# A selective scan in units: one ring of three PSUM tiles for units and side jobs, and stores begun by ScalarE

## What is computed

```
dA = exp(dl[..., None] * A)
h  = dA * h + (dl * ul)[..., None] * Bl[:, :, None, :]
y  = einsum('bkdn,bkn->bkd', h, Cl)      # over 4096 positions in order
```

## Time and profile before

| | |
|---|---|
| median of 3 runs | 11577.95 us (11575.34 to 11589.02) |
| profiled execution | 11574.58 us, its span 11572.8 us |
| first scan, end of last scan | 655.3 us, 9681.1 us |
| busy | VectorE 10116.4, TensorE 9678.0, GpSimd 9157.8, ScalarE 8511.6 us |
| mean granted TensorE clock | 0.957 of 2.4 GHz |

### The profile page before, as it was taken

The page is one execution under the profiler, slowest core; times in us unless marked ns, Lnnn a source line. Parts: engine busy times, 40 slices in busy tenths (PEclk is TensorE's granted clock), DMA queues, the critical chain, the costliest instruction groups (busy, mean ns, idle before and its releaser), DMA issues. The chain is left out here.

```text
span 11572.8 us, 332532 instructions
## 1 busy us (share of the span) xinstructions
PE 9678.0 (84%) x136268; PEld 6104.2 (53%) x136268; DVE 10116.4 (87%) x6303; ACT 8511.6 (74%) x15618; POOL 9157.8 (79%) x3978
## 2 busy tenths in 40 slices
PE   8967888788888788888787778888888887999999
PEld 5644444444444444444444444444444444788778
DVE  7879999999999999999999999999999996555554
ACT  3468888887888788878888888788888884444443
POOL 1169999998999899989999999899999996433330
PEclk9989999999999999999999999999999998999999
DMA  3366676676667766776677666666766674212210
GB/s 103 106 164 169 171 175 171 167 178 168 172 166 174 177 167 164 173 174 168 171 175 178 172 167 171 175 168 171 178 174 166 171 175 111 65 48 67 61 50 12
DMA packets 561649, 1716.32 MB, mean 148 GB/s; under 512 B 147138, under 2 KB 147938, under 8 KB 558344
## 3 DMA queue, kind: packets, MB, share of 16 engines
q1 hardware_dynamic: 560136, 1695.05, 58.4%
HBM read 1319.08 MB, written 375.39 MB: 146 GB/s over the span
## 5 line engine op out<-in xcount | busy, mean ns | idle before, releaser
L975 POOL TENSOR_TENSOR HC<-H,crep 128x1024 f32<-128x1024 f32 x3072 | 7201.2, 2376 | 583.8 <-PE psum L723 416.0
L797 DVE TENSOR_TENSOR_SCAN H<-E,car,psum 128x1024 f32<-128x1024 f32 x2112 | 4868.7, 2336 | 237.4 <-PE psum L701 113.3
L701 PE MATMUL psum<-diag,dluT 128*32 128x128 f32 x98304 | 3350.7, 288 | 1083.0 <-DVE H L797 1049.2
L701 PEld LDWEIGHTS psum<-diag,dluT 128*32 128x32 f32 x98304 | 2852.9, 116 | 2080.8 <-DVE H L797 1887.9
L882 ACT ACTIVATE E<-dlr,am 128x1024 f32<-128x1024 f32 x2816 | 3194.4, 1143 | 1001.7 <-DMA dlr<-scr_dl 519.4
L866 ACT ACTIVATE diag<-idn,blt 128x128 f32<-128x128 f32 x8192 | 2521.6, 389 | 119.8 <-PE psum L701 119.8
L723 PE MATMUL psum<-HC,sely 128*32 128x512 f32 x12288 | 2232.0, 620 | 32.6 <-POOL HC L975 30.9
L775 DVE TENSOR_TENSOR psum<-dur,psum 128x1024 f32<-128x1024 f32 x1280 | 1548.7, 1210 | 114.6 <-PE psum L664 90.4
L797 DVE TENSOR_TENSOR_SCAN H<-E,psum 128x1024 f32<-128x1024 f32 x704 | 1582.1, 2276 | 75.6 <-PE psum L701 45.9
L664 PE MATMUL psum<-sx,selb 96*128 96x512 f32 x2560 | 981.4, 465 | 532.4 <-DVE H L797 522.3
L664 PEld LDWEIGHTS psum<-sx,selb 96*128 96x128 f32 x2560 | 395.4, 190 | 1423.5 <-DVE H L797 1139.3
(11 more groups left out here) (143 smaller groups left out, 9796.9 us busy)
## 6 DMA issues: line engine op xcount, KB each, us to landing
dur<-scr_dlu SPq DMA_DIRECT2D x3072, 128.0 KB, 4.0
dlr<-scr_dl SPq DMA_DIRECT2D x3072, 128.0 KB, 3.8
crep<-scr_bc SPq DMA_DIRECT2D x1024, 256.0 KB, 5.2
scr_dlu<-dlu SPq DMA_DIRECT2D x256, 384.0 KB, 4.6
scr_yk<-yt SPq DMA_DIRECT2D x256, 384.0 KB, 3.0
brep<-scr_bc SPq DMA_DIRECT2D x512, 128.0 KB, 3.5
scr_dl<-dlt SPq DMA_DIRECT2D x128, 384.0 KB, 5.6
scr_dl<-yt SPq DMA_DIRECT2D x128, 384.0 KB, 3.3
```

The source lines that it names most:

```text
L701: r = e.matmul(P[un % 2][32 * q:32 * q + 32, i * 128:(i + 1) * 128], dluT[:, m % 2, i, 32 * j:32 * j + 32], diag[:, i, at + q, :], start=T ...
L797: e.tensor_tensor_scan(H[:, un % NH, ::step], decay[:, ::step], drive[:, ::step], init, ALU.mult, ALU.add).then_inc(scan_done)
L975: e.tensor_tensor(HC[:, un % NHC, :], H[:, un % NH, :], crep[:, GREP.index(g), :], ALU.mult).then_inc(hc_done)
```

## The change

Numbers are per step: x is the unit's place in it, n the step, c the next chunk.

- `yps` moves to the last two banks; the other six make three tiles P[0..2]. A list `ring` writes down the order in which TensorE takes tiles, for units and side jobs alike; a job takes tile (place % 3) and waits until the job three places earlier has released it (a unit by its scan, project by `split`, delta by dl, turn by its copy).
- TensorE fills unit un+2 in iteration un. Side jobs: project at x=4, deltas at 6 and 8 (before 7 and 10), turn at 1 in both steps (odd step before: 0). `turn_b` joins the turn of the even step, its output at column `BLT_AT`.
- ScalarE starts the DMAs of bc (x=6), dl (x=9 and 11 of the even step) and y (x=6) itself; `copy_y` moves from x=4 to 5, the first delta from 7 to 8, the copies of turn from 3 to 2 (even) and 1 to 4 (odd). `DIAGS` is dealt out anew; at the start 32 diags come ahead of exp 0.
- GpSimd's pooled multiply moves from x=11 to 9 (even) and 10 to 11 (odd), its delta of the odd step from 0 to 2.
- u is loaded in two halves of 384 KB, in the odd step after the one whose y is copied.
- SyncE's order is new.

```diff
-    DIAGS = (0, 0, 15, 3, 0, 8, 7, 0, 8, 3, 10, 0, 7, 3, 0, 0, 0, 0, 0, 0, 0, 0, 0, 0)
+    DIAGS = (0, 3, 8, 4, 3, 7, 17, 0, 0, 0, 11, 0, 9, 2, 0, 0, 0, 0, 0, 0, 0, 0, 0, 0)
+    NP = 3
+    BLT_AT = 448
+    FILL_AHEAD = 2
-    P = [psum[:, 0:1024], psum[:, 1024:2048]]
-    yps = psum[:, 2048:3072]
-    stage = psum[:, 3072:4096]
+    P = [psum[:, i * 1024:(i + 1) * 1024] for i in range(NP)]
+    yps = psum[:, 3072:4096]
...
+    def side_jobs(n, x):
         c = n // 2 + 1
+        jobs = []
         if n % 2 == 0:
+            if x == 1:
+                jobs += [("lt", n + 1)]
+            if x == 4 and c < NCHUNK:
+                jobs += [("x", c)]
+            if x == 6 and c < NCHUNK:
+                jobs += [("dt", 2 * c)]
+            if x == 8 and c < NCHUNK:
+                jobs += [("dt", 2 * c + 1)]
+        elif x == 1 and c < NCHUNK:
+            jobs += [("lt", 2 * c)]
+        return jobs
+
+    ring = [("x", 0), ("dt", 0), ("lt", 0), ("dt", 1)] + [("unit", un) for un in range(FILL_AHEAD)]
+    for un in range(NUNIT):
+        if un + FILL_AHEAD < NUNIT:
+            ring += [("unit", un + FILL_AHEAD)]
+        ring += side_jobs(*divmod(un, 12))
+    place_of = {job: i for i, job in enumerate(ring)}
+    released = {"unit": scan_done, "x": sx_split, "dt": dl_made, "lt": lt_copied}
+
+    def bank(*job):
+        return P[place_of[job] % NP]
+
+    def bank_free(e, *job):
+        i = place_of[job] - NP
+        if i >= 0:
+            e.wait_ge(released[ring[i][0]], ring[i][1] + 1)
...
+        def load_rows(b, ci, half):
             t0 = t_of(KORDER[b % 2][0], ci)
+            e.dma_start(u[:, half, t0:t0 + TC], S["xa"][b, half, :, t0:t0 + TC]).then_inc(u_in[half][t0 // TC], 16)
+
+        def next_rows(m, half):
+            b, k, ci, _ = steps[m]
+            if k == KORDER[b % 2][-1] and b + 1 < NB:
+                e.wait_ge(y_copied, m + 1)
+                load_rows(b + 1, ci, half)
...
         for n in range(NSTEP):
             c = n // 2 + 1
             more = n + 1 < NSTEP
             if n % 2 == 0:
                 if more:
-                    in_dlr(n + 1, 1)
+                    in_dur(n + 1, 1)
                     in_dur(n + 1, 0)
+                    in_dlr(n + 1, 0)
                 if n:
                     in_crep(c - 1, 1)
-                    store_y(n - 1)
+                if more:
+                    in_dlr(n + 1, 1)
+                    in_dur(n + 1, 2)
+                    in_dlr(n + 1, 2)
                 load_y(n + 1)
...
-                if c < NCHUNK:
-                    out_bc(c)
-                if more:
-                    in_dlr(n + 1, 2)
-                    in_dur(n + 1, 2)
-                    in_dlr(n + 1, 0)
-                    in_dur(n + 1, 1)
                 if n + 2 < NSTEP:
                     out_dlu(n + 2)
-                    out_dl(n + 2)
-                    out_dl(n + 3)
             else:
                 if more:
                     in_dlr(n + 1, 1)
-                    in_dur(n + 1, 1)
+                if c < NCHUNK:
+                    in_brep(c)
+                if more:
                     in_dlr(n + 1, 0)
                     in_dur(n + 1, 0)
+                    in_dur(n + 1, 1)
+                if n > 2:
+                    next_rows(n - 2, 1)
+                    next_rows(n - 2, 0)
                 if n + 2 < NSTEP:
                     out_dlu(n + 2)
-                store_y(n - 1)
                 load_y(n + 1)
                 if more:
                     in_dur(n + 1, 2)
-                if c < NCHUNK:
-                    in_brep(c)
-                if more:
                     in_dlr(n + 1, 2)
                 if c < NCHUNK:
                     in_crep(c, 0)
...
         def fill(un):
...
-            if un >= 2:
-                e.wait_ge(scan_done, un - 1)
+            bank_free(e, "unit", un)
...
         for un in range(NUNIT + 12):
             n, x = divmod(un, 12)
-            fill(un + 1)
+            fill(un + FILL_AHEAD)
...
+            for job in side_jobs(n, x):
+                side_job(*job)
...
         for un in range(NUNIT + 12):
             n, x = divmod(un, 12)
             c = n // 2 + 1
             ahead(un)
+            if n < NSTEP and n % 2 == 0 and c < NCHUNK:
+                if x == 6:
+                    out_bc(c)
+                if x == 9:
+                    out_dl(2 * c)
+                if x == 11:
+                    out_dl(2 * c + 1)
+            if x == 6 and n:
+                store_y(n - 1)
             if un % 2 == 0 and has_carry(un - 1):
                 carry(un - 1)
-            if x == 4 and n:
+            if x == 5 and n:
                 copy_y(n - 1)
...
```

More of the change, by code:

```diff
@@ L480, in rows_wait @@
         if k == KORDER[b % 2][0]:
[L481 to L485, removed]
+            for h in range(2):
+                e.wait_ge(u_in[h][t_of(k, ci) // TC], 16 * (b + 1))
+    def side_jobs(n, x):
         c = n // 2 + 1
+        jobs = []
         if n % 2 == 0:
[L488 to L493, removed]
+            if x == 1:
[22 more added lines that the diff above has]
+            e.wait_ge(released[ring[i][0]], ring[i][1] + 1)
     def sync(e):
@@ L666, in spread, with turn @@
             return r
-        def turn_b(c):
-            e.wait_ge(*held["bt", c])
-            e.wait_ge(sx_split, c + 1)
-            for k in range(NBLK):
[L672 to L679, removed]
-            for k in range(NBLK // 2):
-                t0 = (sub * (NBLK // 2) + k) * 128
-                r = e.transpose(stage[:, sub * 512 + k * C:sub * 512 + (k + 1) * C], dlu[:, t0:t0 + 128], idn[0:C, 0:C])
-            if sub:
-                r.then_inc(lt_done)
+        def turn(m):
+            o = bank("lt", m)
+            bank_free(e, "lt", m)
+            if m % 2 == 0:
+                e.wait_ge(sx_split, m // 2 + 1)
+                for k in range(NBLK):
+                    e.matmul(o[:, BLT_AT + NDIAG * k:BLT_AT + NDIAG * (k + 1)], sx[0:C, m // 2 % 2, k * 128:(k + 1) * 128],
+                             selt[:], start=True, stop=True)
+            e.wait_ge(dlu_made, m + 1)
+            for k in range(NBLK):
+                at = k // 4 * 512 + k % 4 * C
+                r = e.transpose(o[:, at:at + C], dlu[:, k * 128:(k + 1) * 128], idn[0:C, 0:C])
+            r.then_inc(lt_done)
         def fill(un):
@@ L730, in tensor, with side_job @@
         e.wait_ge(dtw_made, 4)
-        project(0, 0)
-        project(0, 1)
-        delta(0)
-        turn_b(0)
-        turn_dlu(0, 0)
-        turn_dlu(0, 1)
-        delta(1)
-        fill(0)
+        def side_job(name, n):
+            if name == "x":
+                project(n, 0)
+                project(n, 1)
+            elif name == "dt":
+                delta(n)
+            else:
+                turn(n)
+        side_job("x", 0)
+        side_job("dt", 0)
+        side_job("lt", 0)
+        side_job("dt", 1)
+        for un in range(FILL_AHEAD):
+            fill(un)
         for un in range(NUNIT + 12):
             n, x = divmod(un, 12)
-            c = n // 2 + 1
-            fill(un + 1)
+            fill(un + FILL_AHEAD)
             if un >= 5 and (un - 5) % 3 < 2 and (un - 5) // 3 < NG * NSTEP:
@@ L904, in copy_y, with out_dl, out_bc, store_y @@
             e.copy(yt[:], yps[0:C, :]).then_inc(y_copied)
+        def out_dl(m):
+            if m >= 4:
+                for j in range(NJ):
+                    e.wait_ge(dlr_in[slot(m - 4, j)], loaded(m - 4, j))
+            e.wait_ge(dl_made, m + 1)
+            e.dma_start(S["dl"][m % 4], dl[m % 2]).then_inc(dl_out[m % 2], 16)
+        def out_bc(c):
+            if c >= 2:
+                e.wait_ge(crep_in[1], 64 * (c - 1))
+            e.wait_ge(bc_copied, c + 1)
+            e.dma_start(S["bc"][c % 2], bc[NR:NR + NS + 4, :]).then_inc(bc_out, 16)
+        def store_y(m):
+            b, k, ci, half = steps[m]
+            t0 = t_of(k, ci)
+            e.wait_ge(y_copied, m + 1)
+            e.dma_start(S["yk"][b, k % 2, half, :, t0:t0 + TC], yt[:]).then_inc(y_stored, 16)
         e.preload_act_table_set("exp_and_others")
@@ L912, in scalar @@
         project(0)
+        out_bc(0)
         delta(0)
-        turn_b(0)
-        turn_dlu(0)
+        out_dl(0)
+        turn(0)
         delta(1)
+        out_dl(1)
         e.wait_ge(a_made, 2)
+        made = sum(DIAGS[:24 - DIAG_AT])
+        diagonal(0, 0, min(made, 4 * NBLK))
         exp(0)
         exp(1)
-        diagonal(0, 0, sum(DIAGS[:24 - DIAG_AT]))
+        diagonal(0, min(made, 4 * NBLK), max(0, made - 4 * NBLK))
         for un in range(NUNIT + 12):
@@ L931, in scalar @@
             if n % 2 == 0:
[L932 to L933 removed]
+                if x == 2:
+                    turn(n + 1)
                 if x == 5 and c < NCHUNK:
                     project(c)
[L936 removed]
+                if x == 8 and c < NCHUNK:
                     delta(2 * c)
```

110 lines of the change are left out of this document (31 added, 79 removed).

## The result

| | before | after |
|---|---|---|
| median | 11576.65 us (11571.05 to 11589.02) | 11367.69 us (11365.4 to 11374.24) |
| span of the profiled execution | 11572.8 us | 11366.8 us |
| first scan, end of last scan | 655.3, 9681.1 us | 649.7, 9470.3 us |
| mean granted TensorE clock | 0.957 | 0.955 |

The ratio is 0.9818, with a 95% interval of 0.9804 to 0.9833. The predicted 11,320 is 48 us too low. Of the 206.0 us between the spans the loop gives 205.2, the start 5.6, and the end after the last scan takes 4.8 back.

A forecast was written before the change was run, and what follows sets the result against it. VectorE was taken as the bound, working 8621.4 of the scan's 9025.8 us. 8627 + 19 + 3 + 38 + 30 + 51 gave a loop of 8768; with the start, 260 us less in all: about 11,320, range 11,225 to 11,490.

The forecast's parts named there:

- Floor: VectorE's own work in the scan loop: 67.4 us a pair, 8627 us for 128 pairs.
- Ring: TensorE's fills two ahead: VectorE's waits at units 3 and 6 go, while project moves 1.63 us later.
- Split wait: VectorE before the split, waiting for project's copied sx: a stall of 0.15 us a pair, 19 us.
- The GpSimd chain: Project through weigh 6 to scan 6 of the odd step: later weighs cost 3 + 38 + 30 us.
- Allowance: Stalls in the loop that could not be placed: 0.4 us a pair, 51 us.
- Sum: Loop 8768 us, 258 less; with the start 260 less in all, so about 11,320 us.
- Rival A: Project behind scan 4 and the GpSimd chain cost 0.6 to 1.4 us a pair more: 11,390 to 11,500; chance 0.17.
- Signs of being wrong: Runs of four pairs above 280 us, ScalarE DMA issues over 1 us, or VectorE waiting on weighs in plain pairs.
- Stores, queue, u: SyncE's new order ends dlr and carry stalls; five store issues cost ScalarE 0 to 6.3 us a pair, covered by 9.5.
- rival C: ScalarE becomes the bound if a DMA issue holds it past 2.4 us; at 2.6 us 11,680; chance 0.06.
- Rival D: Removed stalls return as waits on GpSimd, its chain +1.63 us in all 128 pairs: within 0.2%; chance 0.04.
- Rival E: Near the floor: GpSimd catches up and the loop's loss terms are at most halved: loop 8698, 11,248 us; chance 0.11.

The follow-up runs named there:

- e9: After, with yp joined to group 1 and dg to group 2 instead of group 0, load_y last in SyncE's lists; 11290.16 us, ratio 0.9746 to before.
- e10: e9 with TensorE's sum ahead of the fill in iterations 2 and 3 of each step; 11238.62 us, ratio 0.9702 to before.
- e1: After's ring, fills and job places, with before's SyncE order, u in one piece and no DMA started by ScalarE; 11618.33 us, ratio 1.0035 to before.
- e7: After, with the stores of bc, dl and y back on SyncE, nearer to where their data are ready; 11368.25 us, ratio 0.9811 to before.
- e8: After, with u loaded in one 768 KB piece in the even step behind load_y; 11369.11 us, ratio 0.9813 to before.
- e2: Before, with only after's SyncE order, u in later halves, and stores begun by ScalarE; 11446.89 us, ratio 0.9885 to before.
- e11: e1 with ScalarE's softplus of the second delta moved from iteration 10 to 9, ahead of exp 12; 11446.09 us, ratio 0.9879 to before.
- e3: Before, with only u loaded in two 384 KB halves in the later odd step; 11511.03 us, ratio 0.9945 to before.
- e6: After, with project moved from x=4 to 6 of the even step, the split to 8, deltas and dlu later; 11411.88 us, ratio 0.985 to before.

## Why the prediction was right, and where it was off

**Floor.** 67.4 us a pair, 8627: VectorE was busy 8612.9 in the loop, 14 us less. It is no fixed floor: in e9 and e10 the same instructions take 8584.

**Ring.** Right on its main point: the fills' waits at 3, 6 and 15 are gone, in e1 as well. Project was to start 0.06 us behind scan 4 and end 3.76 behind it; the medians are 0.055 and 3.76. sx was to be copied at 5.9, and is at 5.84 (median).

**Split wait: the term that was off most in proportion.** 19 us predicted, 45.2 measured. The 0.15 us holds where TensorE keeps up, in 82 of 127 pairs, where project starts within 0.3 us of scan 4's end. In the other 45 it starts up to 1.5 us later, and 40.5 of the 45.2 us stand there. In the pair from 3476.6, fill 5 ran at the lower clock (TensorE, then VectorE, then windows of 4 us and of 1 us, whose last three numbers are clock, DMA share and GB/s):

```profile
3485.76 3.58 PE L696 MATMUL psum<-diag,dluT 128*32 128x128 f32 x64 [0.52 <-DVE H L782]
...
3490.69 3.59 PE L649 MATMUL psum<-u,wx 96*128 96x512 f32 x8
```

```profile
3496.40 1.23 DVE L754 TENSOR_TENSOR sx<-psum,sx 38x1024 fp32r<-38x1024 f32 x1 [1.13 <-ACT sx L817]
```

```profile
3484.00:3488.00 4.00, 3.48 (x52) 2.25 (x54) 3.96 (x3) 4.00 (x11) 4.00 (x3) 0.72 1.04 237
3486.00:3487.00 1.00, 1.00 (x24) 0.94 (x20) 0.96 (x2) 1.00 (x5) 1.00 (x1) 0.50 1.00 229
```

Project starts 1.48 us behind scan 4 instead of 0.05, and the split waits 1.13. In 13 of the 45 pairs fill 5 took over 3 us like this one. e10 leaves one late pair of the 45, and the wait is 8.5 us.

**The GpSimd chain.** 3 + 38 + 30 = 71 us predicted; the waits at units 9, 13 and 18 are 22.8 + 33.4 + 21.4 = 77.6. By kind of pair they are 30.8 for k=3 with yp (38 predicted), 28.8 for yp and dg (30 predicted), and 18.1 for the rest (3 predicted). So the sum is close, but the start of weigh 6 was 8.0, 9.9, 11.75 and is 8.34, 10.36, 12.08 behind scan 4. In the plain pair 0.34 us more lie between project's end and weigh 6 (3292.04 - 3287.45 = 4.59, where the earlier trace rows give 3291.31 - 3287.06 = 4.25). One place of it shows: the fill behind project starts 3.63 us after project's start, where before it was 3.14. The fill is of another kind now, diagonal 7 in place of spread 6; the prediction swapped them at equal price. GpSimd's own part (28.0, 29.1 to 29.4) and VectorE's (29.7 to 29.9) are as worked out. A yp and dg pair shows the end of the chain (GpSimd, then VectorE, then TensorE):

```profile
4788.40 16.33 POOL L989 TENSOR_TENSOR HC<-H,crep 128x1024 f32<-128x1024 f32 x7
4809.31 4.73 POOL L989 TENSOR_TENSOR HC<-H,crep 128x1024 f32<-128x1024 f32 x2 [4.58 <-PE psum L718]
```

```profile
4811.70 2.29 DVE L782 TENSOR_TENSOR_SCAN H<-E,psum 128x1024 f32<-128x1024 f32 x1 [1.61 <-POOL HC L989]
```

```profile
4809.68 1.95 PE L696 MATMUL psum<-diag,dluT 128*32 128x128 f32 x64
```

The scan at 4811.70 is scan 9. The row names GpSimd, since weigh 6 ended just before it (4811.68), but scan 9 needs only weigh 5, the last of the seven that end at 4804.73. What it waits for is fill 9, which ends at 4811.63, 0.07 us ahead of it. All 15 waits at unit 9 are like this (0.07 us behind the fill, 7 us behind weigh 5), while scans that do wait for a weigh start 0.19 us or more behind its end. So the prediction had both the microseconds and the engine right: in these pairs fill 9 is late as well. At 13 and 18 the wait does end with the weigh of four units earlier, 54.8 us in all.

**Allowance.** 51 us; what remains is 207.7 - 45.2 - 77.6 = 85. Of the 207.7 us 142.8 are gaps of 0.15 us or more, which the trace lists, so 64.9 are gaps too short for its list. Before had 348.9 listed of 404, so 55 of the same kind: I counted those 404 as idle that order can win, and then allowed for the short gaps only by what a plain pair's one named wait gave. The listed rest is 20 us, the largest 8.0 at unit 17 behind a fill.

**Sum.** 8627 + 141 = 8768 against 8612.9 + 207.7 = 8820.6: the split wait is 26 short, the chain 7, the allowance 34, the floor 14 too much. The mechanism was right; the split's term was too small because it took TensorE at its best pace, and the allowance because it forgot the short gaps. Rival A describes the first of these; the whole miss is 53 / 128 = 0.41 us a pair, under its lowest price of 0.6.

**Signs of being wrong.** The prediction named three, and each shows a little: three of the four yp and dg runs last 280.2 us and the first run 281.8, 8 of 636 DMA issues on ScalarE take over 1 us, and VectorE waits 5.7 us for weighs in the 32 plain pairs. None is large enough to matter.

**Stores, queue, u.** dlr and carry waits are gone, as said. An issue on ScalarE is short (timeline of ScalarE in after): the median is 0.31 us, so five a pair cost 1.7 us on the mean of an engine that has 9.5 spare, and rival C is out. The y stores have the long ones, up to 1.31 us. SyncE's issues of dl in before have a median of 0.30, so the 1.26 us of the earlier trace rows, the upper end of the prediction's 0 to 6.3 us a pair, was a rare one.

```profile
3288.58 0.28 ACTq L901 DMA_DIRECT2D scr_bc<-dlt  x1
3288.91 0.33 ACTq L907 DMA_DIRECT2D scr_yk<-yt  x1
...
3297.04 0.31 ACTq L895 DMA_DIRECT2D scr_dl<-dlt  x1
```

e7 and e8 add that neither ScalarE's issues nor the halves of u are needed for the gain; SyncE's order is. "No transfer is made faster by this" was not quite so: the dlr loads behind the u pieces landed after 6.6 us in before, and in after the ones next behind u after 3.9. The late dlr loads had two causes, the waits on `copy_y` in all pairs and this transfer in 28.

**What the working missed.** It added the ring's gain and the queue's. Alone the ring costs 47 us (e1) and the queue gives 124 (e2); together they give 209, 132 more than the two added. The reason is the link of e1 and e11, which costs the ring alone 172 us: once delta's tile is in the ring, a late dlr holds an exp, the exp a softplus, and the softplus a unit's fill. (Without the link the two halves give 139 and 124 us and overlap, since 209 is less than their sum.) The prediction's list of who waits for whom had the link (fill 13 for the dl of the second dt job) and gave it no price, since the queue took its cause away. In this change that was harmless; for the ring alone the same working gave a gain, as e1's expectation shows, where the run showed a loss.

**Rival D** (no change) had the chain's +1.63 in all pairs; runs of plain pairs average 67.7 to 68.6 us, so GpSimd's slack there covers it. **Rival E** is what e10 reaches with the further edits of e9 and e10.

## What to carry to other kernels

In a queue that is worked in order, what counts is what stands behind a waiting instruction: SyncE's longest wait in after is longer than before's and costs nothing, and moving the stores to another engine changed nothing once the order was right. Keep a big load that is not urgent away from small urgent ones as well (u and dlr, e3 and e8). Where a trace names the engine that ended a wait, check in the kernel which semaphore value the waiting instruction needs: at unit 9 the engine named had met it 7 us before. A ring shared by units and side jobs gives depth, but ties each unit to the slowest release three places back, so every release must come from an engine that nothing late can hold; measure such a change only together with what it depends on, in both halves. When the critical engine waits on a loop through other engines, look for work that can join a later member of the group (yp in e9) and for the order within one iteration (e10), rather than for a later start of the job (e6 only moved the wait).

## What the hardware showed

- The same 64-matmul fill takes 1.96 us in one pair and 3.58 in another, where the granted clock from 3486 to 3487 us was 0.50 of 2.4 GHz, so 1.2; ahead of it TensorE had idled 0.52 us for a scan, and 1.36 us shortly before that. In e10, with two sums of each step ahead of the fills, the mean clock over the execution is 0.973 against 0.959 in e9, with TensorE's work unchanged. In the loop TensorE is busy 7286 us in place of 7378.
- TensorE's next fill starts 3.63 us after project's start when it is a diagonal one and 3.14 when a spread one, though project lasts 3.70 in both by the model of the trace.
- A DMA issue on ScalarE takes 0.31 us (median of 636 in after's loop; 8 took over 1 us, the longest 1.31). The 127 issues of dl from `dlt` on SyncE in before have a median of 0.30, and 6 took over 1 us, such as the 1.26 of the earlier trace rows.
- In before, dlr loads of 128 KB issued close behind a load of 768 KB landed after 6.6 us (median), other dlr loads after 3.8.
- In VectorE's records a scan overlaps the instruction behind it by 0.08 us (median, after) when that one doesn't wait. A wait costs this overlap as well as its idle time.
